# A linear attention stage by pairs of heads: values projected token-major, the gated product ahead of the square, X kept in DRAM

## What is computed

```
inter = (q_i * q_decay) @ kv
qk    = (q_i @ k_i.T) * diag_decay
intra = qk @ v_i
kv    = block_decay * kv + (k_i * k_decay).T @ v_i
o     = inter + intra
```

## Time and profile before

| | us |
|---|---|
| median of 3 runs | 3098.16 (3093.78 to 3098.34) |
| the profiled execution, its own time | 3093.59 |
| span of its trace | 3091.8 |
| granted TensorE clock, mean over the span | 0.932 |
| normalization lnC, from SP's first load to the next phase's first | 1241.53 to 1277.83 |
| linear attention phase, to the ranking phase's first instruction | 1277.8 to 2760.3 |
| first scores of the linear stage | 1296.28 |
| rest, ranking and kept experts | 2760.3 to 3091.8 |

### The profile page before, as it was taken

How to read it: one execution, slowest core, us unless ns; L and a number is a source line. 1 busy time by engine, 2 the same in 40 slices (tenths; PEclk the granted TensorE clock), 3 DMA queues, 4 the chain that set the end, 5 groups by cost and what they waited for, 6 DMA issues and landing times. The chain is left out here.

```text
span 3091.8 us, 51426 instructions
## 1 busy us (share of the span) xinstructions
PE 2803.0 (91%) x17564; PEld 2237.6 (72%) x17564; DVE 1804.6 (58%) x3284; ACT 1466.3 (47%) x2689; POOL 793.4 (26%) x812
## 2 busy tenths in 40 slices
PE   5689999979889999599999999999999999978573
PEld 4534444448668888488888888988888898868452
DVE  5378888826678887555555555555555545556421
ACT  5337777766468877433333333333333333334110
POOL 2412212210052222022222222222222222214675
PEclk9879999999989999699999999999999999975575
DMA  4875655230064543000000000000000000002376
GB/s 145 238 102 75 84 69 74 30 94 3 4 224 186 189 177 136 23 11 0 10 10 10 10 10 3 8 10 10 10 10 10 0 10 10 8 27 88 90 173 123
DMA packets 159113, 193.65 MB, mean 63 GB/s; under 512 B 18257, under 2 KB 135537, under 8 KB 150257
## 3 DMA queue, kind: packets, MB, share of 16 engines
q1 hardware_dynamic: 150464, 177.10, 21.9%
q0 software_dynamic: 8544, 15.22, 2.9%
HBM read 149.89 MB, written 46.58 MB: 64 GB/s over the span
## 5 line engine op out<-in xcount | busy, mean ns | idle before, releaser
L744 DVE TENSOR_REDUCE score_pm<-score_SM 128x1 f32<-128x512 f32 (+3 forms) x608 | 364.2, 655 | 124.1 <-PE score_SM L613 73.3
L1718 POOL TENSOR_TENSOR lin_o2sum<-lin_o2sum,lin_o 128x512 f32<-128x512 f32 x128 | 165.8, 1296 | 1049.2 <-ACT lin_o L1754 1049.2
L1933 DVE SCALAR_TENSOR_TENSOR lin_go<-lin_gT,lin_O 128x512 f32<-128x512 f32 x128 | 88.0, 688 | 477.0 <-ACT lin_o L1754 477.0
L704 ACT ACTIVATE score_PR<-score_SE 128x512 f32<-128x512 f32 (+1 forms) x640 | 309.9, 557 | 106.0 <-PE score_SE L638 102.6
L1789 PE MATMUL lin_PJ<-C_XH,lin_WH 128*128 128x512 f32 x1032 | 342.6, 413 | 13.1 <-DVE lin_WL L1893 13.1
L1789 PE MATMUL lin_PJ<-C_XL,lin_WH 128*128 128x512 f32 x1032 | 322.6, 394 | 0.0
L1789 PE MATMUL lin_PJ<-C_XH,lin_WL 128*128 128x512 f32 x1032 | 321.3, 393 | 0.0
L1950 DVE TENSOR_TENSOR C_acc<-lin_OUT,C_acc 128x512 f32<-128x512 f32 x256 | 177.0, 692 | 142.0 <-PE lin_OUT L1824 139.6
L610 PE MATMUL score_SM<-score_KR,score_QR 96*128 96x512 bf16 (+3 forms) x768 | 230.2, 341 | 28.2 <-DMA score_V<-v_rows 25.5
L1737 ACT ACTIVATE lin_qT<-lin_PJ 128x512 f32<-128x512 f32 x129 | 76.9, 596 | 376.2 <-PE lin_PJ L1789 376.2
L1789 PEld LDWEIGHTS lin_PJ<-C_XH,lin_WL 128*128 128x128 f32 x1032 | 194.3, 188 | 44.9
(11 more groups left out here) (351 smaller groups left out, 6398.7 us busy)
## 6 DMA issues: line engine op xcount, KB each, us to landing
experts_sq<-B_roots SPq DMA_DIRECT2D x64, 1024.0 KB, 4.7
score_QR<-q_parts SPq DMA_DIRECT2D x96, 128.0 KB, 7.1
score_KR<-k_parts SPq DMA_DIRECT2D x96, 128.0 KB, 7.7
kept_GU<-L_ffn_gate_up_proj SPq DMA_DIRECT2D x48, 192.0 KB, 3.1
v_rows<-qkv_vt SPq DMA_DIRECT2D x32, 256.0 KB, 2.6
score_V<-v_rows SPq DMA_DIRECT2D x16, 512.0 KB, 10.8
C_w<-L_attn_w_qkv SPq DMA_DIRECT2D x51, 128.0 KB, 2.3
q_parts<-qkv_parts SPq DMA_DIRECT2D x16, 384.0 KB, 2.6
```

The source lines that it names most:

```text
L704: nc.scalar.activation(PR[:, st % BUFS, h, 0:width], SE[:, e % RING, 0:width], ACT.Exp, scale=SCALE)\
L744: nc.vector.tensor_reduce(pm[:, n % 2, h0:h0 + nh, t, k0 // CHUNK], SM[:, count % RING, 0:nh * nk].rearrange("p (h k) -> p h k", h=nh), AX ...
L1718: nc.gpsimd.tensor_tensor(o2sum[:, c], o2sum[:, c], o2[:], ALU.add).then_inc(pool_sum, 1)
```

## The change

1. The loop runs over 8 pairs of heads; in it over chunks, and in each chunk over the two heads j = 0, 1. Weights, decays and states of two heads are held, and loaded and split per pair. Steps are still 128.
2. V is projected token-major for both heads at once: the activations are the stationary side (128 positions), the weights of two heads stream (256 columns), two sequences per call of `project_v`, one call per step. The transposes into VT and ScalarE's copy are gone; the SiLU writes v directly. V has a PSUM bank of its own, VP; G goes to Q's bank.
3. go waits for O itself, the square for go, the next O for the square. On ScalarE `goh` comes ahead of the square.
4. X is stored to DRAM (`x_rows`) among lnC's prefetches, and C_acc takes its place in SBUF. The first run of 8 tiles comes back during the linear phase, the other three at the ranking phase's start.

```diff
-        vT = ph.sb("vT", [P, B4, BLK])
-        v = ph.sb("v", [P, B4, DH])
+        v = ph.sb("v", [P, 2, B4, 2 * DH])
...
+            sp.dma_start(x_first, x_rows[0:RT * P, :].rearrange("(t p) n -> p t n", p=P)).then_inc(x_in, 16)
...
-            def vg(n, u):
-                act.wait_ge(pe_v, done(n))
-                nc.scalar.activation(vT[:], PJ[:, 0], ACT.Silu).then_inc(act_v, 1)
+            def values(m, slot, half):
+                act.wait_ge(pe_v, done(m))
+                nc.scalar.activation(v[:, slot, 2 * half:2 * half + 2, :], VP[:], ACT.Silu).then_inc(act_v, 1)
+
+            def gates(n, u):
                 act.wait_ge(dve_go, done(n - 2))
                 act.wait_ge(pe_g, done(n))
 
-                nc.scalar.activation(gT[:, u], PJ[:, 1], ACT.Tanh, scale=0.5).then_inc(act_g, 1)
-                act.wait_ge(pe_vt, done(n))
-                nc.scalar.activation(v[:], VT[:], ACT.Copy).then_inc(act_vt, 1)
+                nc.scalar.activation(gT[:, u], PJ[:, 0], ACT.Tanh, scale=0.5).then_inc(act_g, 1)
 
             def square(i):
-                act.wait_ge(pe_o, done(i))
+                act.wait_ge(dve_go, done(i))
...
+                    if (c, j) != (LAST, 1):
+                        qk(i + 1, 1 - j)
+                        gated_high(i)
                         square(i)
+                        if c < LAST:
+                            values(g * TURNS + 2 * (c + 1) + j, (c + 1) % 2, j)
+                        gates(i + 1, 1 - j)
+                    else:
+                        weights_high(g + 1)
                         gated_high(i)
-                    else:
-                        weights_high(h + 1)
                         square(i)
-                        gated_high(i)
-                        qk(i + 1, 1 - u)
-                    vg(i + 1, 1 - u)
+                        qk(i + 1, 0)
+                        values(i + 1, 0, 0)
+                        gates(i + 1, 0)
+                        values(i + 2, 0, 1)
...
-            def project_qk(n, c, load):
-                if c == 0:
+            def project_qk(n, c, j, load):
+                if (c, j) == (0, 0):
                     pe.wait_ge(wl_ready, 2 * load + 1)
-                pe.wait_ge(act_v, done(n - 1))
-                project(0, Q, c, pe_q)
                 pe.wait_ge(act_g, done(n - 1))
-                project(1, K, c, pe_k)
-
-            def project_vg(n, c, load):
+                project(0, Q, c, j, pe_q)
+                pe.wait_ge(act_k, done(n - 1))
+                project(1, K, c, j, pe_k)
+
+            def project_g(n, c, j):
+                pe.wait_ge(act_q, done(n))
+                project(0, G, c, j, pe_g)
+
+            def project_v(m, c, half, load):
                 if c == 0:
                     pe.wait_ge(wl_ready, 2 * load + 2)
-                pe.wait_ge(act_q, done(n))
-                project(0, V, c, pe_v)
-                pe.wait_ge(act_k, done(n))
-                project(1, G, c, pe_g)
-
-                pe.wait_ge(act_v, done(n))
-                pe.wait_ge(act_vt, done(n - 1))
-                for b in range(B4):
-                    ins = nc.tensor.transpose(VT[:, b, :], vT[:, b, :], ident[:])
-                ins.then_inc(pe_vt, 1)
-
-            def output(i, h):
+                pe.wait_ge(act_v, done(m - 1))
+                for b in range(2):
+                    n = 0
+                    for x, a in ((xh, WH), (xl, WH), (xh, WL)):
+                        for k in range(KD):
+                            ins = nc.tensor.matmul(VP[:, b, :], x[:, k, 2 * half + b, c, :], a[:, V, k, :],
+                                                   start=(n == 0), stop=(n == 3 * KD - 1))
+                            n += 1
+                ins.then_inc(pe_v, 1)
...
-                    if c < NBLK - 1:
-                        project_qk(i + 1, c + 1, h)
-
-                    pe.wait_ge(act_vt, done(i))
+                    if (c, j) != (LAST, 1):
+                        project_qk(i + 1, c + j, 1 - j, g)
+
+                    pe.wait_ge(act_v, done(g * TURNS + 2 * c + 1))
                     pe.wait_ge(dve_sd, done(i))
                     pe.wait_ge(pool_qd, done(i))
-                    pe.wait_ge(dve_go, done(i - 1))
+                    pe.wait_ge(act_sq, done(i - 1))
                     for b in range(B4):
-                        ins = nc.tensor.matmul(O[:, b, :], v[:, b, :], sd[:, b, :], start=True, stop=(c == 0))
+                        ins = nc.tensor.matmul(O[:, b, :], v[:, c % 2, b, j * DH:(j + 1) * DH], sd[:, b, :],
+                                               start=True, stop=(c == 0))
                         if c:
-                            ins = nc.tensor.matmul(O[:, b, :], kv[:, b, :], qd[:, b, :], start=False, stop=True)
+                            ins = nc.tensor.matmul(O[:, b, :], kv[:, j, b, :], qd[:, b, :], start=False, stop=True)
                     ins.then_inc(pe_o, 1)
                     pe.wait_ge(dve_kd, done(i))
-                    if c < NBLK - 1:
+                    if c < LAST:
                         for b in range(B4):
-                            ins = nc.tensor.matmul(KT[:, b, :], kd[:, b, :], v[:, b, :], start=True, stop=True)
+                            ins = nc.tensor.matmul(KT[:, b, :], kd[:, b, :], v[:, c % 2, b, j * DH:(j + 1) * DH],
+                                                   start=True, stop=True)
                         ins.then_inc(pe_kv, 1)
-                        project_vg(i + 1, c + 1, h)
-                        output(i, h)
+                        project_v(g * TURNS + 2 * (c + 1) + j, c + 1, j, g)
+                    if (c, j) != (LAST, 1):
+                        project_g(i + 1, c + j, 1 - j)
+                        output(i, g, j)
                     else:
 
-                        project_qk(i + 1, 0, h + 1)
-                        output(i, h)
-                        project_vg(i + 1, 0, h + 1)
+                        project_qk(i + 1, 0, 0, g + 1)
+                        project_v(i + 1, 0, 0, g + 1)
+                        output(i, g, j)
+                        project_g(i + 1, 0, 0)
+                        project_v(i + 2, 0, 1, g + 1)
...
                         .then_inc(dve_kd, 1)
-                    if c == NBLK - 1:
-                        weights_low(h + 1, 0)
-                        weights_low(h + 1, 1)
-
-                    dve.wait_ge(act_sq, done(i))
+                    if (c, j) == (LAST, 1):
+                        weights_low(g + 1, 0)
+                        weights_low(g + 1, 1)
+
+                    dve.wait_ge(pe_o, done(i))
                     dve.wait_ge(act_g, done(i))
                     dve.wait_ge(dve_gol, done(i - 1))
...
+                  (x_rows.rearrange("(t p) n -> p t n", p=P), X[:]),
...
+            for r in range(1, RUNS):
+                sp.dma_start(x_of(r * RT, RT), x_rows[r * RT * P:(r + 1) * RT * P, :].rearrange("(t p) n -> p t n", p=P))\
+                    .then_inc(x_in[r - 1], 16)
...
+                if run:
+                    dve.wait_ge(x_in[run - 1], 16)
                 for t in tiles:
-                    nc.vector.scalar_tensor_tensor(X[:, t, :], acc[:, t, :], rs[:, t:t + 1], X[:, t, :],
-                                                   ALU.mult, ALU.add).then_inc(x_ready, 1)
+                    xt = x_of(t)[:, 0, :]
+                    nc.vector.scalar_tensor_tensor(xt, acc[:, t, :], rs[:, t:t + 1], xt, ALU.mult, ALU.add)\
+                        .then_inc(x_ready, 1)
                 for t in tiles:
...
-        acc = keep("C_acc", [P, TILES, D])
+        acc = nc.alloc_sbuf_tensor_at("C_acc", [P, TILES, D], F32, offset=x_at)
```

More of the change, by code:

```diff
@@ L11 @@
+import itertools
 from contextlib import ExitStack
@@ L1704, in _ @@
             give_credit(pool, pool_qd, pool_sum)
-            with pool.Fori(0, H) as h:
-                for c in range(NBLK):
-                    i, u = h * NBLK + c, c % 2
+            with pool.Fori(0, HP) as g:
+                for c, j in itertools.product(range(NBLK), range(2)):
+                    i = g * TURNS + 2 * c + j
                     pool.wait_ge(act_q, done(i))
@@ L1722, in _ @@
             act.preload_act_table(ACT.Silu)
-            give_credit(act, act_q, act_k, act_v, act_g, act_vt, act_sq, act_goh)
+            give_credit(act, act_q, act_k, act_v, act_g, act_sq, act_goh)
             def weights_high(load):
                 act.wait_ge(w_in, (load + 1) * 64)
-                act.wait_ge(pe_g, done(load * NBLK - 1))
-                for pair in PAIRS:
+                act.wait_ge(pe_g, done(load * TURNS - 1))
+                act.wait_ge(pe_v, done(load * TURNS - 1))
+                for pair in PARTS:
                     nc.scalar.activation(WH[:, pair], raw[:, pair], ACT.Copy).then_inc(wh_ready, 1)
@@ L1788, in project @@
                     for k in range(KD):
-                        ins = nc.tensor.matmul(PJ[:, bank], a[:, w, k, :], x[:, k, :, c, :],
```

(31 more changed lines are left out.)

195 lines of the change are left out of this document (102 added, 93 removed).

## The result

| | before | after |
|---|---|---|
| median, us | 3096.02 (4 runs) | 3048.08 (3047.2 to 3050.63, 4 runs) |
| the profiled execution | 3093.59 | 3047.91 |
| linear stage, SP's first DMA to the ranking stage's first instruction | 1482.44 | 1434.73 |
| first scores to last scores | 1438.65 | 1388.96 |

The ratio of the times is 0.9846 (95% interval 0.9829 to 0.9864): 47.9 us less. In the two profiled executions the stage alone lost 47.7 us, so all of the gain lies where it was looked for. The rest of the program became 1.2 us shorter ahead of the stage and 3.2 us longer in the kept experts behind it, which leaves 45.7 us between these two executions.

What follows compares the result with a forecast made beforehand. TensorE's instruction stream was taken to bound the linear stage. 8 pairs x (-5.3 - 0.95) = -50.0, start +1.6, small splits +0.5 gave -48 us: 3045.3 from 3093.6, with 3047 forecast as median, range 3036 to 3070.

Steps and rivals of the forecast that it cites:

- V, -0.38 us a step: Ordinary linear-stage step on TensorE: token-major V without transposes makes V, G and output 4.34 instead of 4.72 us.
- Last chunk: A pair's two last steps: 22.03 instead of 22.98 us, -0.95 a pair, including a new 1.0 us stall on gol.
- third rival: Smaller gain: 0.1 to 0.2 us waits at re-ordered hand-overs, or DMA terms at bad ends; 3056 to 3072, chance 0.16.
- The order of go and square: Ordinary step: go ahead of the square removes no time itself, but covers 1.2 us of waiting for gol.
- The lock: Rival: gol issued after o2sum waits for GpSimd, +50 or +190 us (3097 or 3237); full form within slower, 0.07.
- mild form: gol waits for o2sum only: output at 8.5 instead of 8.07, time 3097; chance 0.03 together with no change.
- Loads that show: Rival: V's weight loads run at the recorded 188 ns, not hidden behind matmuls; +99 us, 3146; within slower, 0.07.
- some 4 us better: Pricing V's two halves by the skill page, 6 ns above one whole, would improve the sum by some 4 us.
- X in DRAM, 0: X's store hidden during normalization, loads at the ranking stage's start: 0, at most +3; store +12 at half rate.
- The split of the weights: A pair's weights split in 1024-column pieces, 1.22 us against 0.68: nothing, or +1 us over the kernel.
- Start, +1.6: Linear stage's start: first weight split 0.54 longer, half block of V 1.4 ahead of first scores, less 0.35 of transposes.

## Why the prediction was right, point by point

- *V, -0.38 us a step.* Measured -0.42 (11.41 to 10.99) for the twelve steps of a pair in chunks 1 to 6, and 10.11 and 10.09 for the two of chunk 0 without the jump (10.69 before, twice; 0.17 of that is the order of go, by the run with the order alone). V came at 1.51 us for the 1.50 taken from the output's rows. This sum is 12 x 0.42 + 2 x 0.59 = 6.2 a pair instead of 5.3, and 0.3 of it is the order of go.
- *Last chunk.* The last-but-one step was put at 9.86 with a stall of 0.98 and took 9.78 with a stall of 0.83 between TensorE's matmuls (1.00 as the prediction counts it, from start to start: 2.48 from G to the output, less 1.48). The last step was put at 12.17; written out it is 12.18, and with the loop 13.28 on the mean of seven. **This is the step that failed**: the sum has nothing for the loop's jump, though "a program twice as long in the loop" stands in the third rival as a reason for some 0.1 to 0.2 us. By the runs above it costs (13.28 - 12.18) + (10.31 - 10.11) = 1.30 us a jump, 9.1 over seven.
- The two misses nearly cancel, and that is luck. A pair's steps sum to 175.3 us against 181.25 before, -5.9 where -6.25 was predicted; without the jump it is -7.2 (174.0). The time came out close because the gain in the other steps was larger than priced and hid a cost that had not been looked for.
- *The order of go and square.* "Removes no time by itself" holds for the ordinary steps of the kernel before; at the heads' ends it removes 10 us over the program. As a cover it was put at 1.2 us and gol is done 1.16 before the output. What it covers was under-priced: without it the changed kernel loses 72 us, since gol then meets qd, where the prediction speaks only of a wait and gives no price.
- *The lock* as a rival did not come: gol took 679 to 693 ns in all 128 steps. It was near, though: gol leads o2sum by 0.32 us in the step shown and by 0.23 to 0.53 over all steps, where 0.5 was estimated. The experiment with the square first shows the lock: its ordinary steps are 0.43 us longer, as the rival's mild form has them (8.5 instead of 8.07), but with the pairs' ends the time is 3120, not 3097.
- *Loads that show*: V's starts are 0.12 apart, not 0.188.
The rows have 0.117 x 2 - 0.231 = 3 ns, so page and rows agree on the price of splitting a matmul, and "some 4 us better" does not follow. (The sum, too, gives 3045.7 where 3045.3 stands.) Nothing rests on either.
- *X in DRAM, 0*. The normalization took 36.30 us in both, and the DMA engines, at 342 GB/s from 1250 to 1260 us, are at 0 from 1260 us on, long before its end at 1276.6. The three loads at the ranking stage's start landed in 6.2, 8.8 and 11.0 us and VectorE came to the second run of rows 10.34 us behind the ranking stage's start in both profiles. Only the traces show this; no run undoes this part by itself.
- *The split of the weights*: pieces of 1024 took 1.22 us as the earlier trace rows had it, and no wait of TensorE names them behind the first.
- *Start, +1.6.* From the stage's first DMA to the first scores +1.4 (18.45 to 19.84).

The wait of the engines at the jump is shown, by the loops written out and by two heads in the old loop. That it has to do with fetching instructions is read from the packets: none come at the jumps of the 8-step body, which costs next to nothing, and they come at those of the 16-step body. No run sets the length of the body apart from the fetching. Why TensorE waits 0.7 to 1.2 us at its jump in the changed kernel and 2.9 to 3.3 with the old V in the same loop (packets 146 and 145) stays open. What stands ahead of the jump differs: with the old V transposes that wait for ScalarE, now matmuls of G and V. Whether that is it was not tested.

## What to carry to other kernels

Price a matmul by the nearest row of its own form, and a longer loop body as a change of its own: look for "issue" at the first instructions behind the jump on every engine, since one engine's late start can lie hidden beside another's. Before moving an operation away from a shared resource, ask who takes the resource next; here a lead of 0.2 to 0.5 us stands ahead of 48 us. An edit that gains little alone (10 us here) can be what lets another one gain (72 us): try them apart and together.

## What was not expected of the hardware

- A loop body of 8 steps of the linear stage costs VectorE 0.2 us at the jump back and TensorE nothing that the waits show; one of 16 steps costs 2.8 to 3.3 us on VectorE and 0.7 to 3.3 on TensorE, every time.
- VectorE's one-input scaling in fp32 took 4.53 us instead of 0.35 beside GpSimd's clearing of a buffer, which reads nothing, and ended with it; a subtraction of two tensors beside the same kind of clearing kept its 1.2 us. This was seen once.
- With the first projection 5.6 us earlier in the stage, TensorE worked at the granted clock of 0.50 for 6.08 us instead of 4.47, and 0.7 us of the gain went there.
- The 64 matmuls of one column at the stage's end, the same in all versions, took 9.9 to 12.5 us from version to version. Gains of 1 to 2 us in the stage can be lost or found there; the cause was not looked for.
